# A transformer layer on one core: another order for tiles 11 to 31 on TensorE, ScalarE and VectorE, and k of tile 10 turned on TensorE

## The reference

```python
x = _layernorm(x + attn(x))            # q, k with rotary; v; g = silu(x @ Wg)
x = _layernorm(x + ffn(x))             # (silu(x @ wg.T) * (x @ wu.T)) @ wd.T
# attn, in chunks of 64 rows, per head with decay gamma:
attn = einsum('bhid,bhjd->bhij', qb, kb) * D
o    = attn @ vb + (qb * cross_q) @ S
S    = gC * S + (kb * cross_k).T @ vb
out  = (rmsnorm(o) * gn * g) @ Wo
```

## Time and profile before

| What | Value |
|---|---|
| median of 3 runs | 437.25 us (436.45 to 441.94) |
| the profiled execution's own time | 433.49 us |
| its span | 431.7 us |
| mean granted TensorE clock | 0.994 |
| TensorE weight loads (PEld), busy | 381.8 us, 88% |
| VectorE (DVE), busy | 337.3 us, 78% |
| ScalarE (ACT), busy | 257.6 us, 60% |
| GpSimd (POOL), busy | 185.0 us, 43% |

### The profile page before, as it was taken

How to read it: one execution, slowest core, us unless ns; L and a number is a source line. 1 busy time by engine, 2 the same in 40 slices (tenths; PEclk the granted TensorE clock), 3 DMA queues, 4 the chain that set the end, 5 groups by cost and what they waited for, 6 DMA issues and landing times.

```text
span 431.7 us, 12808 instructions
## 1 busy us (share of the span) xinstructions
PE 406.5 (94%) x4574; PEld 381.8 (88%) x4574; DVE 337.3 (78%) x974; ACT 257.6 (60%) x810; POOL 185.0 (43%) x330
## 2 busy tenths in 40 slices
PE   8999999998979999999999999999999999979895
PEld 6899999998969899888899988889998899879894
DVE  4989677678857888878888888888898788836775
ACT  5668655576655566665556566555766655533551
POOL 1422343445424553444454344545434443423654
PEclk9999999999999999999999999999999999989999
DMA  8921010100313334344333434433443343310001
GB/s 269 372 116 51 0 52 2 64 0 26 81 46 82 85 94 109 85 104 111 75 93 94 111 81 106 111 70 91 101 110 85 84 105 76 76 37 14 14 24 54
DMA packets 86577, 36.26 MB, mean 84 GB/s; under 512 B 68336, under 2 KB 79472, under 8 KB 86512
## 3 DMA queue, kind: packets, MB, share of 16 engines
q1 hardware_dynamic: 86368, 35.34, 31.4%
q10 hardware_dynamic: 144, 0.07, 0.1%
HBM read 23.07 MB, written 12.32 MB: 82 GB/s over the span
## 4 chain that ended last, share of the span: by engine, by line
PE 51%; DVE 17%; DMA 10%; issue 9%; POOL 6%; SPq 5%; ACT 1%; POOLq 0%; DVEq 0%; ACTq 0%
PE b_ffn L600 16%; PE b_rows L600 14%; PE b_rows L618 9%; POOL rs L2262 4%; DMA k_rows<-wf_int 3%; SPq L535 3%; DMA wf_int<-y_rows 2%; DMA y_rows<-wf_int 2%; SPq L549 2%; POOL ve L2260 2%; DVE st L1913 2%; DVE wo_raw L1929 2%; PE b_head L804 1%; PE b_rows L614 1%; DVE z L1911 1%
## 5 line engine op out<-in xcount | busy, mean ns | idle before, releaser
L2242 POOL TENSOR_TENSOR h_lo<-wf_int,h_hi 128x256 fp32r<-128x256 f32 x96 | 70.6, 739 | 91.3 <-ACT h_hi L1337 91.3
L600 PE MATMUL b_ffn<-x1T_hi,wf_hi 128*128 128x256 f32 x384 | 94.6, 286 | 7.0 <-DVE x1T_lo L1828 6.7
L600 PE MATMUL b_ffn<-x1T_lo,wf_hi 128*128 128x256 f32 x384 | 91.9, 279 | 0.0
L600 PEld LDWEIGHTS b_ffn<-x1T_hi,wf_hi 128*128 128x128 f32 x384 | 72.7, 189 | 12.5 <-DVE x1T_lo L1828 11.6
L600 PEld LDWEIGHTS b_ffn<-x1T_lo,wf_hi 128*128 128x128 f32 x384 | 72.8, 190 | 0.0
L618 PE MATMUL b_rows<-wp_hi,xT_lo 128*128 128x256 f32 x244 | 66.8, 278 | 0.0
L618 PE MATMUL b_rows<-wp_hi,xT_hi 128*128 128x256 f32 x230 | 64.4, 280 | 1.2 <-issue 1.2
L618 PE MATMUL b_rows<-wp_lo,xT_hi 128*128 128x256 f32 x230 | 64.0, 278 | 0.0
L1337 ACT CAST h_hi<-wf_int 128x256 fp32r<-128x256 f32 x96 | 38.7, 406 | 41.4 <-DVE wf_int L1767 41.4
L2252 POOL TENSOR_TENSOR ms_eps<-ms,eps 128x4 f32<-128x4 f32 x32 | 7.0, 217 | 105.8 <-ACT sq L1313 105.6
L600 PE MATMUL b_rows<-wf_hi,h_hi 128*128 128x256 f32 x192 | 46.9, 283 | 0.1
(11 more groups left out here) (200 smaller groups left out, 1163.2 us busy)
## 6 DMA issues: line engine op xcount, KB each, us to landing
y_rows<-wf_int SPq DMA_DIRECT2D x20, 256.0 KB, 2.3
wf_int<-y_rows SPq DMA_DIRECT2D x80, 64.0 KB
xT_raw<-in_xT SPq DMA_DIRECT2D x16, 256.0 KB, 3.7
x_sb<-in_x SPq DMA_DIRECT2D x16, 256.0 KB, 3.5
out<-wf_int SPq DMA_DIRECT2D x30, 128.0 KB, 2.9
k_rows<-wf_int SPq DMA_DIRECT2D x22, 128.0 KB, 2.3
qkT<-k_rows SPq DMA_DIRECT2D x88, 32.0 KB, 2.3
wf_int<-in_w_ffn SPq DMA_DIRECT2D x6, 384.0 KB, 6.7
```

The lines of the kernel that those rows point to most:

```text
L600: mm = pe.matmul(dst, a, b, start=(i == 0 and j == 0 and not begun), stop=(i == n - 1 and j == len(passes) - 1 and not more), skip_group_c ...
L2242: pool.tensor_tensor(h_lo[:, ring, hb], h_full[:, u], h_hi[:, ring, hb].bitcast(F32), ALU.subtract).then_inc(h_split[j], 1)
```

## The change

On TensorE, from slot 11 on, the heads come right behind the projections of q and k; x1 is turned behind the heads; then v; gate blocks 0 and 1; down; block 2; attention output; the gate projection. Before, x1 was turned ahead of the heads, v came behind block 1 and down behind block 2. `turn_qk` in these slots waits for a smaller count of `yT_split`. In the drain `down` goes ahead of `turn_y`, and gate block 2 ahead of `attention_out`.

k of tile 10 is now turned on TensorE: `moved` excludes it, and the counts of the semaphores follow (`blocked`, `turned_before`).

On ScalarE the copy of v in slot 10 goes ahead of the squares; in slot 11 `keep_qk` and `split_x1T` go first; from slot 12 on `split_x1T` moves behind `turn_q` 0, `turn_q` 1 right behind the squares, and gate 1 ahead of the copy of v. On VectorE `split_x1T` moves behind the two sums of the state; sines and `add_q` behind the mask; `residual_2` ahead of `gated_output`; `residual_1` and `moments_1` ahead of hidden 2, `stats_2` and `moments_2`. GpSimd's program is not changed; SyncE's changes only in its counts and in tile 10.

```diff
         def moved(n):
-            return PACKED <= n < NT - 1
+            return PACKED <= n < NT - 1 and n != TURNED - 1
...
                     if s >= PACKED:
-                        pe.wait_ge(yT_split, s - 2)
+                        pe.wait_ge(yT_split, min(s, TURNED) - 2)
...
@@ -1093,21 +1098,21 @@
                 keys_and_queries(s, q, t)
+                heads_ready(s)
+                heads(s)
                 if s > TURNED:
                     turn_x1(*at(s - 4, X1T_LAG))
-                heads_ready(s)
-                heads(s)
+                project(s, q, t, 1, v_done)
                 gate_up_block(*at(s, -1), 0, wide)
                 gate_up_block(*at(s, -1), 1, wide)
...
-                project(s, q, t, 1, v_done)
-                gate_up_block(*at(s, -1), 2, wide)
                 if has_q(s, t):
                     pe.wait_ge(k_parts, s - NATURAL + 1)
                 down(*at(s - 7, DOWN_LAG), wide, free=(rot_parts, s + 1))
+                gate_up_block(*at(s, -1), 2, wide)
                 attention_out(*at(s - 3, 2), free=(v_copied, s + 1))
                 project(s, q, t, 2, g_done)
@@ -1134,11 +1139,11 @@
+                down(*at(NT - 6, DOWN_LAG), wide, (0,), begun=True)
                 turn_y(*at(NT - 1, 2))
-                down(*at(NT - 6, DOWN_LAG), wide, (0,), begun=True)
                 gate_up_block(*at(NT, 0), 1, wide)
+                gate_up_block(*at(NT, 0), 2, wide)
                 attention_out(*at(NT - 1, 2), free=(z2_ready, NT - 5))
-                gate_up_block(*at(NT, 0), 2, wide)
@@ -1403,13 +1408,18 @@
-                if s > PACKED:
+                if s > PACKED and s < TURNED - 1:
                     mean_squares(*at(s - 2, 1))
                 copy_v(s, q, t)
+                if s == TURNED - 1:
+                    mean_squares(*at(s - 2, 1))
@@ -1489,20 +1499,23 @@
+                if s == TURNED:
+                    keep_qk(s, q, t)
+                    split_x1T(*at(s - 4, X1T_LAG))
                 gate_v(*at(s, -1))
                 if exists(s + 3):
                     split_xT(*at(s, 3))
-                if exists(s - 4):
+                turn_q(s, q, t, 0)
+                if s > TURNED:
                     split_x1T(*at(s - 4, X1T_LAG))
-                turn_q(s, q, t, 0)
                 mean_squares(*at(s - 2, 1))
+                turn_q(s, q, t, 1)
                 gate(b, tb, 0)
-                split_y(*at(s - 3, 2))
                 if not moved(s):
                     keep_qk(*at(s, 1))
-                turn_q(s, q, t, 1)
+                split_y(*at(s - 3, 2))
+                gate(b, tb, 1)
                 copy_v(s, q, t)
-                gate(b, tb, 1)
@@ -2024,28 +2037,28 @@
+                add_first_half(s - 1)
+                add_second_half(s - 1)
                 if s > TURNED:
                     split_x1T(*at(s - 4, X1T_LAG))
-                add_first_half(s - 1)
-                add_second_half(s - 1)
                 sum_k(s, q, t)
                 if moved(s):
                     block_k(s)
                 mask(*at(s - 1, 1))
+                turned_sines(s, q, t)
+                add_q(s, q, t)
                 hidden(b, tb, 0)
                 split_y(*at(s - 3, 2))
+                residual_2(*at(s - 7, DOWN_LAG))
                 gated_output(*at(s - 2, 1))
                 if moved_y(s - 2):
                     block_y(s - 2)
                 hidden(b, tb, 1)
-                residual_2(*at(s - 7, DOWN_LAG))
-                stats_2(*at(s - 7, DOWN_LAG))
-                hidden(b, tb, 2)
-                moments_2(s - 7, (s - 7) % TS)
-                turned_sines(s, q, t)
                 residual_1(*at(s - 3, 2))
                 moments_1(s - 3)
-                add_q(s, q, t)
+                hidden(b, tb, 2)
+                stats_2(*at(s - 7, DOWN_LAG))
+                moments_2(s - 7, (s - 7) % TS)
```

More of the change, by code:

```diff
@@ L332, in moved, with blocked @@
         def moved(n):
-            return PACKED <= n < NT - 1
+            return PACKED <= n < NT - 1 and n != TURNED - 1
+        def blocked(n):
+            return sum(moved(i) for i in range(n + 1))
         def moves(n):
-            return 16 * (P // BLOCK) * (n - PACKED + 1)
+            return 16 * (P // BLOCK) * blocked(n)
         def turned_before(n):
-            return min(n, PACKED)
+            return sum(not moved(i) for i in range(min(n, NT - 1)))
         def packed_rows(s, k):
@@ L523, in write_k @@
             def write_k(n):
-                sp.wait_ge(k_blocked, n - PACKED + 1)
+                sp.wait_ge(k_blocked, blocked(n))
                 sp.dma_start(k_rows, k_blocks).then_inc(k_written, 16)
@@ L835, in turn_y @@
                         pe.wait_ge(next_kept, nexts_to(TURNED - 1))
+                        pe.wait_ge(qkT_kept, turned_before(TURNED - 1) + 1)
                     if n + 3 > PACKED:
@@ L1405, in packed_slot @@
                 split_h(b, tb, 1)
-                gate(b, tb, 2)
+                if s > PACKED:
+                    gate(b, tb, 2)
                 turn_q(s, q, t, 0)
                 turn_q(s, q, t, 1)
+                if s == PACKED:
+                    gate(b, tb, 2)
                 split_h(b, tb, 2)
-                if s > PACKED:
+                if s > PACKED and s < TURNED - 1:
                     mean_squares(*at(s - 2, 1))
                 copy_v(s, q, t)
+                if s == TURNED - 1:
+                    mean_squares(*at(s - 2, 1))
             def early_slot(s, q, t):
@@ L1676, in sum_k @@
                     if not moved(s - 2):
-                        dve.wait_ge(qkT_done, s - 1)
+                        dve.wait_ge(qkT_done, turned_before(s - 2) + 1)
                     if s - 2 >= CHUNKED:
```

2 lines of the change are left out of this document (1 added, 1 removed).

## The result

The changed kernel takes 457.7 us (median of 4 runs, 456.4 to 458.4), the kernel before on the same chip 438.06 (4 runs, 436.45 to 441.94). The ratio is 1.043, 95% interval 1.036 to 1.051: slower. The forecast was 463 with a range of 449 to 478. The profiled execution took 457.5 us, its span is 455.9 against 431.7.

What follows compares the result with a forecast made beforehand. The prediction took a loop of waits through VectorE, GpSimd and ScalarE as the bound. 433.5 - 0.9 + 32.3 - 4.2 - 1.1 = 459.6, and 3.8 for the median over the profiled execution gave 463 us, range 449 to 478.

Steps and rivals of the forecast that it cites:

- The bound: Every tile: a loop of waits through VectorE, GpSimd and ScalarE, not TensorE, sets the period of 12.50 us.
- Mark to norm_2: VectorE, from residual_1's add (the mark) to norm_2: powers wait behind hidden 2's split; 2.95 to 4.43 us, 1.48 more.
- Rotate_q to mask: VectorE's piece from rotate_q to mask: ScalarE's moved cast of x1 delays the squares; 2.89 to 3.26 us, 0.37 more.
- Mask to the next mark: VectorE's piece from mask to the next residual_1: stats_2, hidden 2, moments_2 leave, add_q enters; 5.20 to 5.06 us.
- The periods: The 19 tiles between the marks at 133.22 and 371.79: 1.7 us more each, +32.3 us.
- TensorE's new order at nothing: TensorE's reordering covers its own gaps but costs or gains nothing, since it would wait for VectorE's split of x1.
- Tiles 10 and 11: Up to the mark at 133.22: TensorE's 2.56 us wait goes, later squares cost about 1.9; -0.9 us.
- The last tile: After the mark at 371.79: turn_qk's smaller yT_split count removes TensorE's 2.99 us wait; -4.2 us, bounds -2 and -4.5.
- Drain: Kernel end: down and gate block 2 fill TensorE waits of 0.63 and 1.12 us, entry loses up to 0.8; -1.1 us.
- the first rival: Clock falls in every tile from TensorE's stop ahead of gate block 0, 0.8 to 0.9 us each: 478 us; chance 0.12.
- TensorE as the bound: Second rival: TensorE bounds, v ahead of gate block 0 closes its gaps; period 11.6, 412 us; chance 0.07.
- The third rival: VectorE's waits merely change places, nothing more up to norm_2, +0.2 a tile: 435 us, no change; chance 0.07.

Runs made afterwards that it cites:

- e1_powers_first: Changed kernel with GpSimd's two inv_std (powers) moved ahead of its third split_h; 429.87 us, ratio 0.988 to the kernel before.
- e3_cast_first: Changed kernel with ScalarE's cast of x1 put back ahead of the first turn of q; 449.2 us, ratio 1.032 to the kernel before.
- e6_squares10: Changed kernel with ScalarE's old order in tile 10, squares ahead of the copy of v; 455.63 us, ratio 1.054 to the kernel before.
- e7_wait_only: Kernel before with only the yT_split count relaxed for the turn of q and k in tile 31; 431.31 us, ratio 0.994.
- e5_all: Changed kernel with GpSimd's powers ahead of the third split, ScalarE's x1 cast ahead of turn_q, VectorE's norm_2 behind the state adds; 424.8 us, ratio 0.985.

## Why the prediction was right

- *The bound.* The step that decided it was not to take the busiest engine for the bound. The loop through VectorE, GpSimd and ScalarE set the period, and e1_powers_first showed it by an edit on the engine that is busy for 40% alone. "Perfetto Trace Analysis", section Identifying the Most-Contended Engine, in the Trainium skill would have the engine with the highest occupancy improved first, here TensorE. By these runs TensorE does not set the period of the changed kernel.
- *Mark to norm_2* (+1.48 forecast): +1.36 measured, and 1.33 by e1_powers_first. Rows 5 from the drain gave the chain almost to the length: 222.64 + 0.85 - 220.19 = 3.30 from hidden 2 to norm_2 against the 3.42 there.
- *Rotate_q to mask* (+0.37): +0.26, and 0.28 by e3_cast_first. I counted the cast's duration; the squares start 0.27 behind its start, and that step is what counts (226.14 to 226.41).
- *Mask to the next mark* (5.06): 4.90. From mask to hidden 0 it was 1.47, where my terms give 0.40 + 0.13 + 0.44 + 0.35 = 1.32, the waits a bit too small. The rest was 0.3 shorter than 5.20 - 0.40 - 0.75 - 0.31 = 3.74: a part is that residual_2 is no longer followed by the stats that read it, a step of 0.33 and not 0.46 (207.23 to 207.69 before).
- *The periods.* 17 of them at +1.3 where 1.7 was forecast, the sum of these three small excesses, and two falls of the clock at 1.55 each, which I had put into a rival. +26.98 against +32.3: the mechanism held, but without the 3.1 us of the two falls the periods give +23.9, so the step of 1.7 a tile was a third too high.
- *TensorE's new order at nothing:* right for the whole change, but for a reason that I had only half. I named its wait ahead of gate block 0 as cover, and it is; but alone the order costs 0.68 a tile by the uncovered wait at the down projection, which I hadn't looked for.
- *Tiles 10 and 11* (-0.9, bounds -2.6 and +1): +1.05, just outside. The order of the squares cost 1.73 where the step said 1.9 (a stop of 2.64). Two terms were off: without that order the start gains only 1.44 (e6_squares10), so the end of the 2.56 us wait was not worth its length, and I had put no fall of the clock behind the stop, 0.76 more.
- *The last tile* (-4.2): -3.98, with e7_wait_only as proof of the cause.
- *Drain* (-1.1): +0.15, wrong. The two waits of the earlier trace rows were filled (the first is gone, the second is 0.39), and it moved nothing: from mark to mark the drain's next two stretches are 14.55 together before (403.12 - 388.57) and 14.61 after (427.23 - 412.62), and norm_2 follows by 6.67 (409.79) and 6.66 (433.89). I counted filled waits of TensorE in a stretch that another chain sets, the very mistake that I had avoided in the tiles.
- *Luck in the sum.* The periods came out 5.3 us below their forecast, tiles 10 and 11, the last tile and the drain together 3.4 above theirs, and 3.1 of the periods' 26.98 are falls of the clock that belong to the first rival. That the whole span is within 2 us of the sum (+24.2 against +26.1) is in part luck.
- *The rivals.* The clock fell, but in 2 of 19 tiles, and there the tile paid the whole 1.55 us and not 0.8 to 0.9: no slack of TensorE took any of it. TensorE as the bound is excluded for this kernel, and even e5_all, with 0.6 of waiting left, is 0.7 a tile above 11.6. The third rival fails by the 1.50 ahead of norm_1.

## What to carry to other kernels

When an instruction is moved on one engine, look up where the engine that serves it has it in its own order: here VectorE's moments were moved ahead of hidden 2 and GpSimd's powers stayed behind hidden 2's split, and that mismatch alone was worth 1.33 us a tile. An order is good or bad only with those of its neighbours: the same exchange on TensorE gained 0.4 to 0.8 us a tile with the old orders of VectorE, ScalarE and GpSimd, and lost 1.9 with the ones of e5_all. And a filled wait of the busiest engine is a gain only where a mark on the path moves with it.
